# Second normalised rows turned by VectorE blocks and device memory instead of TensorE, in a graph layer with a mixer and eight experts

## The reference, cut to what matters

```python
N = 6250; D = 256; E = 8
xn = layernorm(x)                                   # x: (6250, 256)
g  = graph_layer(xn, edges)                         # attention weights times gathered rows
m  = mixer(xn)                                      # linear attention over all rows, then gelu(ret @ w1 + b1) @ w2 + b2 + xn
x2 = x + g + m
z  = layernorm(x2)                                  # the "second normalised rows"
w  = softmax(mean(z) @ Wr + br)                     # one sample, so mean(z) is z: 8 weights per row
h1 = relu(bn1(z  @ W1[e] + b1[e]))                  # for each of 8 experts e, 256 by 256
h2 = relu(bn2(h1 @ W2[e] + b2[e]))
out = x2 + sum_e w[:, e] * (h2 @ Wo[e] + bo[e])
```

## Time and profile before

| | |
|---|---|
| time, 3 runs | 1104.52, 1103.9, 1102.42 us; median 1103.9 |
| span of the profiled execution | 1101.4 us |
| what a run takes beyond that span (median less span) | 2.5 us |
| PE busy / PE weight loads / DVE / ACT / POOL | 99% / 89% / 68% / 67% / 22% |

### The profile page before, as it was taken

One profiled execution on the slowest core, in us unless ns is written; L12 is line 12 of the kernel. 1 busy time (PEld: TensorE's weight loads), 2 busy tenths in 40 slices (PEclk: granted clock), 3 DMA queues, 4 the chain that ended last, 5 costly groups with the idle time before them and its releaser, 6 DMA issues.

```text
span 1101.4 us, 19301 instructions
## 1 busy us (share of the span) xinstructions
PE 1092.1 (99%) x6656; PEld 979.2 (89%) x6656; DVE 752.0 (68%) x1752; ACT 735.4 (67%) x1275; POOL 247.1 (22%) x287
## 2 busy tenths in 40 slices
PE   9999999999999999999999999999999999999998
PEld 7988988989888888888898888888888988889998
DVE  7888756776576675775765766757657657666565
ACT  5777757775675766666756757666667566666665
POOL 4787753312012021030120120210301201100000
PEclk9999999999999999999999999999999999999999
DMA  6877851211011110110110111101101101100000
GB/s 187 262 233 253 233 187 34 59 40 49 1 50 49 39 49 11 39 59 1 49 49 6 45 49 39 50 11 39 59 1 49 49 12 33 35 20 1 1 21 15
DMA packets 71300, 67.92 MB, mean 62 GB/s; under 512 B 20641, under 2 KB 66579, under 8 KB 71203
## 3 DMA queue, kind: packets, MB, share of 16 engines
q1 hardware_dynamic: 66552, 59.34, 17.8%
q0 software_dynamic: 3968, 6.71, 2.4%
q10 hardware_dynamic: 683, 0.64, 0.2%
HBM read 40.87 MB, written 25.80 MB: 61 GB/s over the span
## 4 chain that ended last, share of the span: by engine, by line
PE 92%; POOL 3%; issue 2%; DVE 2%; ACT 1%; DMA 0%; DVEq 0%; POOLq 0%; ACTq 0%
PE bank L280 29%; PE bank L281 28%; PE bank L282 28%; PE bank L985 1%; POOL gathered L597 1%; PE bank L1152 1%; PE bank L1164 1%; PE bank L1162 1%; PE bank L926 1%; PE bank L918 1%; PE bank L1180 0%; POOL gathered L615 0%; POOL alpha_l L617 0%; PE bank L942 0%; DVE sum_squares L1337 0%
## 5 line engine op out<-in xcount | busy, mean ns | idle before, releaser
L1381 DVE SCALAR_TENSOR_TENSOR accumulated<-bank,router_w,accumulated 128x256 f32<-128x256 f32 (+2 forms) x392 | 170.4, 479 | 199.3 <-PE bank L282 192.8
L661 ACT ACTIVATE h<-weight_stage 128x512 fp32r<-128x512 f32 (+2 forms) x206 | 113.5, 598 | 196.8 <-PE bank L282 177.4
L282 PE MATMUL bank<-ffn_w_high,h 128*128 128x256 f32 (+2 forms) x778 | 220.0, 283 | 0.0
L280 PE MATMUL bank<-ffn_w_high,h 128*128 128x256 f32 (+2 forms) x778 | 219.7, 282 | 0.2 <-DVE h L1231 0.2
L281 PE MATMUL bank<-ffn_w_low,h 128*128 128x256 f32 (+2 forms) x778 | 219.9, 283 | 0.0
L1231 DVE TENSOR_TENSOR h_low<-activated,h_high 128x512 fp32r<-128x512 f32 (+2 forms) x208 | 135.3, 657 | 79.4 <-ACT h_high L661 75.7
L812 ACT ACTIVATE activated<-bank,bn_cols 128x512 f32<-128x512 f32 (+2 forms) x208 | 156.3, 751 | 48.5 <-PE bank L282 45.1
L812 ACT ACTIVATE weight_stage<-bank,bn_cols 128x512 f32<-128x512 f32 (+2 forms) x208 | 154.2, 751 | 47.7 <-PE bank L282 46.2
L280 PE MATMUL bank<-xT_high,ffn_w_high 128*128 128x512 f32 (+2 forms) x416 | 159.5, 383 | 0.1
L280 PE MATMUL bank<-h_high,ffn_w_high 128*128 128x512 f32 (+2 forms) x416 | 157.8, 379 | 0.0
L281 PE MATMUL bank<-xT_low,ffn_w_high 128*128 128x512 f32 (+2 forms) x416 | 157.3, 378 | 0.0
(11 more groups left out here) (226 smaller groups left out, 1940.0 us busy)
## 6 DMA issues: line engine op xcount, KB each, us to landing
x_rows<-in_x SPq DMA_DIRECT2D x18, 512.0 KB, 4.8
x_turned<-xT_high SPq DMA_DIRECT2D x22, 256.0 KB, 3.6
x_turned<-xT_low SPq DMA_DIRECT2D x22, 256.0 KB, 4.5
out<-accumulated SPq DMA_DIRECT2D x11, 512.0 KB, 3.3
mix_xT_high<-x_turned SPq DMA_DIRECT2D x10, 512.0 KB
mix_xT_low<-x_turned SPq DMA_DIRECT2D x10, 512.0 KB
weight_stage<-in_L_ffn_W SPq DMA_DIRECT2D x16, 256.0 KB, 3.0
node_table<-gathered SPq DMA_DIRECT2D x22, 132.0 KB, 2.9
```

The source lines that it names most:

```text
L280: nc.tensor.matmul(dst, ah, bh, start=(k == 0), stop=False)
L282: last = nc.tensor.matmul(dst, al, bh, start=False, stop=(k == n - 1))
L661: return nc.scalar.activation(dst, src, ACT.Copy)
L1381: last = V.scalar_tensor_tensor(a, y_of(ch, e)[b][0:tp, (t % 2) * D:(t % 2 + 1) * D], wts(ch)[0:tp, t, e:e + 1], a, ALU.mult, ALU.add)
```

## The change

For the ten chunks with number 2 to 11 (512 rows each) z is no longer turned by TensorE. VectorE turns each 32 by 32 block in place in the step before (`x2_blocks`, one STREAM_TRANSPOSE of 128 by 1024 from `normalised` into `residual`), SyncE stores the result to device memory (`norm_blocks`, 512 KB) and, when the store has landed, loads it back with the blocks exchanged, in 8 transfers of 32 partitions with runs of 32 numbers. The loads land in `normalised`, seen as `xnT`. `x2_high` and `x2_low` read it there in place of `Fb`. `x2_norm` and `x2_blocks` now stand ahead of `hid2` of step 4; `x2_high` moves from the end of step 5 to step 6 ahead of `relu2`, and `x2_low` from the end of step 5 to step 6 behind `accumulate`. Chunks 0, 1 and 12 keep TensorE. `router` stays in step 6.

```diff
+        def by_dma(ch):
+            return ch.c >= 2 and ch.rows == CH
...
+            def turn_rows(ch):
+                n = turned_by_dma(ch)
+                need(sp, s["fxs"], n)
+                sp.dma_start(nt_d[n % 2], base[:, :, :]).then_inc(s["nst"], 16)
+                need(sp, s["nst"], 16 * n)
+                for b in range(P // Q):
+                    for k in range(KT):
+                        cb = (k * P + b * Q) // Q
+                        block = nt_d[n % 2].rearrange("(q i) t (c j) -> c i t q j", i=Q, j=Q)[cb]
+                        sp.dma_start(xnT[b * Q:(b + 1) * Q, k, :].rearrange("p (t q j) -> p t q j", t=TPC, j=Q),
+                                     block).then_inc(s["nld"], 16)
...
+                if not ch.last and by_dma(ch.next()):
+                    turn_rows(ch.next())
...
             def x2_high(ch):
                 for k in range(KT):
-                    need(act, s["f2T"], KT * ch.c + k + 1)
+                    if by_dma(ch):
+                        need(act, s["nld"], 16 * 2 * (P // Q) * turned_by_dma(ch))
+                    else:
+                        need(act, s["f2T"], KT * (turned_by_pe(ch) - 1) + k + 1)
...
-            FRONT = {0: base_shift, 1: gnn_exp, 2: gelu, 5: x2_high, 6: router_exp}
+            FRONT = {0: base_shift, 1: gnn_exp, 2: gelu, 6: router_exp}
...
+                    if nxt is not None and by_dma(nxt) and e == 6:
+                        x2_high(nxt)
                     relu2(ch, e)
+                    if nxt is not None and not by_dma(nxt) and e == 5:
+                        x2_high(nxt)
...
-                    elif nxt is not None and e in FRONT and not (ch.c == 0 and e == 3):
+                    elif nxt is not None and e in FRONT and not (ch.c == 0 and e == 3) and not (by_dma(nxt) and e == 5):
                         FRONT[e](nxt)
...
+            def x2_blocks(ch):
+                need(dve, s["fx2n"], ch.c + 1)
+                V.transpose(base[:, :, :], xn[:, :, :]).then_inc(s["fxs"], 1)
...
+            FRONT_D = {**FRONT, 4: (), 5: ()}
...
+                    if nxt is not None and by_dma(nxt):
+                        if e == 4:
+                            x2_norm(nxt)
+                            x2_blocks(nxt)
+                        elif e == 6:
+                            x2_low(nxt)
                     if not (ch.last and e == NE - 1):
                         hid2(ch, e)
```

More of the change, by code:

```diff
@@ L104, in build @@
         al_d = tab_d.rearrange("n (b h) -> (n b) h", h=GH)
+        nt_d = nc.dram_tensor("norm_blocks", (2, P, TPC, D), fp32).ap()
         xt_d = nc.dram_tensor("x_turned", (NC, 2, P, KT, CH), fp32).ap()
@@ L151, in build @@
         gelx = xn[:, :, :].rearrange("p (h a) d -> p h (a d)", h=2)
+        xnT = xn[:, :, :].rearrange("p (k a) d -> p k (a d)", k=KT)
         Gt = G[:, :].rearrange("p (t n) -> p t n", t=TPC)
@@ L210, in build @@
             m_blk m_sum m_t m_q m_kv m_p m_pv m_pa m_m m_hi m_lo m_c m_cb w1_sum w1_ev b1_new wq_sum bq_new
-            rsl xB0 xB1 xst0 xst1 xst2 xm fxa fxn gmsg gln xmB fm1 gelu gelh fmh fm2 fx2 fst frs fx2n f2T f2hi f2lo frt flg fex fw3 fw3T fw3c fbo fai
+            rsl xB0 xB1 xst0 xst1 xst2 xm fxa fxn gmsg gln xmB fm1 gelu gelh fmh fm2 fx2 fst frs fx2n f2T f2hi f2lo fxs nst nld frt flg fex fw3 fw3T fw3c fbo fai
             idx0 idx1 blk gath0 gath1 glog gexp0 gexp dsm
@@ L320, in h2_free, with turned_by_dma, turned_by_pe @@
                 need(eng, s["y"], NE * ch.b0 + ch.nb * e)
+        def by_dma(ch):
+            return ch.c >= 2 and ch.rows == CH
+        def turned_by_dma(ch):
+            return sum(by_dma(c) for c in CHUNKS[:ch.c + 1])
+        def turned_by_pe(ch):
+            return sum(not by_dma(c) for c in CHUNKS[:ch.c + 1])
         def gathered(ch):
@@ L852, in gelu @@
                     need(act, s["fm1"], 2 * ch.c + h + 1)
-                    if ch.c != 1:
+                    if ch.c > 2:
+                        need(act, s["f2lo"], KT * ch.c)
+                    elif ch.c != 1:
                         need(act, s["f2T"], KT * ch.c)
@@ L871, in x2_high @@
                         need(act, xst(newest(ch)), turned_stored(newest(ch)))
-                    copy(xTh[:, ch.par, k, 0:ch.rows], Fb[k][:, 0:ch.rows]).then_inc(s["f2hi"], 1)
+                    full = xnT[:, k, :] if by_dma(ch) else Fb[k][:, 0:ch.rows]
+                    copy(xTh[:, ch.par, k, 0:ch.rows], full).then_inc(s["f2hi"], 1)
             def router_exp(ch):
@@ L1399, in base_rows @@
                 need(dve, s["fxa"], ch.c + 1)
+                if ch.c > 2:
+                    need(dve, s["nst"], 16 * turned_by_dma(ch.prev()))
                 V.tensor_tensor(base_of(ch)[0:tp, 0:nt, :], xb[0:tp, ch.par, 0:nt, :],
@@ L1493, in x2_low @@
                         need(dve, xst(newest(ch)), turned_stored(newest(ch)))
-                    low(xTl[:, ch.par, k, 0:ch.rows], Fb[k][:, 0:ch.rows], xTh[:, ch.par, k, 0:ch.rows]).then_inc(s["f2lo"], 1)
+                    full = xnT[:, k, :] if by_dma(ch) else Fb[k][:, 0:ch.rows]
+                    low(xTl[:, ch.par, k, 0:ch.rows], full, xTh[:, ch.par, k, 0:ch.rows]).then_inc(s["f2lo"], 1)
             def route(ch):
@@ L1585, in _ @@
                     if nxt is not None:
-                        for step in (FRONT_1 if nxt.c == 1 else FRONT).get(e, ()):
+                        for step in (FRONT_1 if nxt.c == 1 else FRONT_D if by_dma(nxt) else FRONT).get(e, ()):
                             step(nxt)
```

## The result

The changed kernel takes 1137.49 us (median of 4 runs, 1136.47 to 1137.83) against 1103.45 for the kernel before; ratio 1.0305, 95% interval 1.0290 to 1.0319. The forecast was 1119, range 1113 to 1150. The direction and the wait came out as forecast; the size did not: 34 us instead of 15, and the reason is the clock.

The account below looks back on a forecast made before the run. TensorE, busy 99% of the span, was taken to bound the kernel. Per chunk +2.4 us of router wait less 0.88 of transposes gave +1.5, ten chunks +15: span 1116.4, with 2.5 for the median 1119, range 1113 to 1150.

Parts of the forecast that it names:

- What bounds the kernel: TensorE, busy 99% of the span: its queue's losses and gains move the end; work saved on other engines is worth nothing.
- The gain of the spared transposes: TensorE's queue ahead of L1: eight transposes cost 0.88 us a chunk by spacing, 8.8 us for ten chunks.
- The prediction's rival with 272 ns a transpose: TensorE's transposes cost more than their spacing: at 272 ns each ten chunks gain 22 us against 24 of waits, 1102; chance 0.04.
- Step 4 on VectorE: x2_norm and a 1.2 us block transpose ahead of hid2 leave L3 margins of 1.2 and 1.0 us: nothing to pay.
- The transfer: Store and eight loads through device memory land at 658, hidden up to 659.8, so by 1.8 us.
- The wait at the router: TensorE's router behind L3 of expert 5 waits for x2_low, now behind accumulate on VectorE: 2.4 us a chunk.
- The clock falls in the wait: During TensorE's 2.4 us pause the clock drops to the 1.2 GHz level, losing 1.2 us a chunk: 1131; chance 0.08.
- The base case: Router wait of 2.4 us a chunk with the transfer hidden: 1119, own range 1113 to 1125; chance 0.62.
- loads that land late: Loads landing beyond 659.8 delay x2_high, each us later costing 10 us: 1151 or 1203; chance 0.25.

Follow-up runs that it names:

- no turning at all: Kernel before, with z of chunks 2 to 11 not turned by any means, so their result is not the reference's: 1094.94 us, ratio 0.9924.
- nine equal filling products: Changed kernel with nine identical unused products of 512 columns in TensorE's queue ahead of the router's wait: 1132.16 us, ratio 1.0264.
- `x2_norm` late: Changed kernel with x2_low ahead of accumulate, and x2_norm and the block transpose back behind hid2 of step 4: 1102.20 us, ratio 0.9993.
- the wait filled to the end: Changed kernel with eleven unused products ahead of the router's wait, lasting longer than the wait for x2_low: 1119.49 us, ratio 1.0150.
- The run with pauses of 2.9 us: Changed kernel with the router behind the next chunk's first L1 and x2_low behind hid2 of step 6: 1134.74 us, ratio 1.0301.
- the wait alone: Kernel before, TensorE's transposes kept and no transfer added, only x2_low of chunks 2 to 11 moved behind accumulate in step 6: 1154.49 us, ratio 1.0464.
- five filling products: Changed kernel with five unused products ahead of the router's wait: 1136.83 us, ratio 1.0302.
- with `x2_low` first: Changed kernel with x2_low ahead of accumulate in step 6 on VectorE: 1094.86 us, ratio 0.9927.
- varied filling: Changed kernel with nine unused products ahead of the router's wait, each with other weights and columns: 1131.35 us, ratio 1.0242.
- the run with two routers: Changed kernel with x2_low ahead of accumulate, and the router's products of chunks 2 to 11 issued twice: 1127.03 us, ratio 1.0219.

## Why the prediction was wrong

**What bounds the kernel: right.** What TensorE's queue lost was paid in full, and nothing caught up.

**The gain of the spared transposes: right.** 0.88 us a chunk by spacing; 0.82 with no turning at all (8.2 us in ten chunks). The 390 ns of the Trainium skill, VectorE: DVE Perf Modes, "The three transpose paths", would have made 31 us of it, by estimate; the runs show a quarter of that. The prediction's rival with 272 ns a transpose has a slip: 1103.9 + 24 - 22 is 1106, not 1102.

**Step 4 on VectorE: right.** The block transpose took 1.25 us (1.2 taken), and the list of waits has L3 waiting for `hid2` once, 0.2 us, as in the kernel before.

**The transfer: right that it is hidden, 1.8 us too late in size.** The store lands in 2.6 us (3.5 taken) and a packet takes 0.013 us (0.018 taken). The rule of 512 bytes from the Trainium skill, DMA: Bandwidth & Descriptors, table "Specifications", spoke for a late landing. By the packet the trace agrees that short ones move below the full rate: 128 bytes in 0.013 us are 10 bytes a nanosecond for one engine, against 4 KB in 0.195 us, 21, in the earlier trace rows. Whether they are read and modified first, no run here shows. At half the pace 512 KB were still back in time.

**The wait at the router: right.** 2.17 us of empty engine, 2.44 lost by the time L1 goes on; 2.4 taken. The run of the kernel before with `x2_low` moved has the same 21.7 us.

**The clock: the step that failed.** The text had it as a rival, "The clock falls in the wait" with 0.08, at 1.2 us a chunk and 1131. The base case put the clock's term at nothing, because in 172:176 a pause of 1.6 us took nothing. TensorE's timeline there:

```profile
174.10 0.63 PE L1152 MATMUL bank<-identity,normalised 120*128 120x120 f32 x4 [1.53 <-DVE normalised L1485]
174.57 0.84 PE L918 MATMUL bank<-ones 128*128 128x128 f32 x6
175.52 0.35 PE L280 MATMUL bank<-xT_high,ffn_w_high 128*128 128x240 f32 x1
```

The pause is 1.53 us, shorter than the new wait, and products of 120 and 128 columns follow. It was also one sample: with the same code, the clock did fall at this place, at 175 us, in two of the later profiled kernels (nine equal filling products, and `x2_norm` late). So the row showed that the clock can hold there, not that it does. At the router the wait has 1.8 us of products of 16 and 8 columns right behind. The runs show a stretch of little work, 2.17 + 1.81 = 4.0 us, with which it fell ten times in ten. With the wait filled to the end the clock held in all ten chunks, and 3.5 us of thin products without any wait brought it down in eight. With full products between wait and router it held too, but there the pause was only 1.66 us; a pause of 2.17 us with nothing thin behind it was not run. The products of 16 and 8 columns show as busy in the profile, so neither the busy share nor the list of waits tells that the stretch goes on. The price was low as well: 1.7 us a piece, and two pieces in two chunks, 2.0 a chunk in place of 1.2.

That 1137 lies in the stated range of 1113 to 1150 is luck. The base case had 1113 to 1125, and the part above was put there for loads that land late; they landed early.

With the clock kept the base case is 1103.5 - 8.8 + 24.4 = 1119, as forecast; the run that fills the wait to the end, with 2.5 us of products a chunk in place of the 2.4, is at 1119.5. The Trainium skill, TensorE: Matmul & The Clock Gate, section "Why this matters for your kernels", warns against idle gaps of the engine between bursts of products. The run with pauses of 2.9 us agrees in five chunks of ten; the runs add falls behind thin products, where there was no gap.

## What to carry to other kernels

When a piece moves on one engine, look what its consumer stands behind on the other engine, and what the piece now stands behind: here `x2_low` was put behind an `accumulate` that needed the very products ahead of the router, so the wait was certain from the code, and moving it two lines up, into an idle stretch, turned 34 us of loss into 8 us of gain. Price a pause of TensorE together with the thin products on either side of it, and look at the granted clock after it, since 20 of the 34 us lost here stood in products that were not waiting at all. The transposes that the change spares were worth a tenth of a microsecond each; a list that gives them 272 ns each overstates such a gain more than twofold.

## What was not expected of the hardware

- TensorE's granted clock falls behind stretches without wide products, whether the engine is empty or busy with products of 16 and 8 columns. How often in the profiled executions, by the stretch: 4.0 us of both, ten times in ten (the changed kernel, and the wait alone); 3.5 us of thin products, 8; 3.0 us of both behind five filling products, 10; 2.9 us of pause, 5, strictly every second; 2.6 us of both, 4; 2.1 us of both behind nine filling products, 8 in each of two runs; 1.7 us of thin products (the kernel before, with `x2_low` first, without turning, with eleven filling products), none; 1.66 us of pause, none. In the run with `x2_norm` late five chunks had 2.2 to 2.9 us of both, and none fell.
- Longer stretches mostly fall more often, but the length does not decide alone: 2.1 us behind filling products fell in 8 of 10 and 2.6 us without any in 4. What else decides stays open. The counts are not ten independent trials: in the changed kernel, where one piece is lost, the next fall comes 78.5 us later while the chunks come 78.7 apart, so it slides against the work from chunk to chunk, from 2.9 us after the router's first product to 1.3. That, and the strict alternation at 2.9 us, would fit something periodic, but no run tests it. Other executions of a kernel can fall a different number of times: with varied filling three had a mean clock of 0.987 or 0.988 and one 0.992.
- The moment of the fall varies: in the changed kernel 1.3 to 2.9 us after work had begun again, in the run with two routers 0.2 to 1.3 us after the wide products had, and with pauses of 2.9 us some 0.2 to 0.6 us before they ended. It stays down for about 3.4 us or twice that, so the loss comes in pieces of up to 1.7 us.
- Packets of 128 bytes cost 0.013 us of a DMA engine, about as much as the 0.012 that bounds those of 4 bytes in the earlier trace rows; 4096 of them over 16 engines are 3.3 us of each engine's time, less than the 5.3 us that SyncE takes to issue the eight transfers, so here the issue probably set the pace.
- At 172 to 176 us, where the code is the same in all these kernels, the clock held in most profiled runs and fell in two, for 6.8 us each; in two others (no turning, and the router late with the longer pause) it fell 9 to 10 us after the start, for 3.4 us. A kernel can therefore differ by 1.7 to 3.4 us from another in a stage that neither touches.
